# A graph network's gathered tiles: who begins them, who squares the mean, who adds the update products

## The reference

```python
msg = jnp.concatenate([h[src], h[dst]], axis=-1) @ Mw.T + Mb
s1 = jax.ops.segment_sum(msg, dst, num_segments=N)
s2 = jax.ops.segment_sum(msg * msg, dst, num_segments=N)
mx = jax.ops.segment_max(msg, dst, num_segments=N)
mn = jax.ops.segment_min(msg, dst, num_segments=N)
mean = s1 / degc
var = jax.nn.relu(s2 / degc - mean * mean)
std = jnp.sqrt(var + STD_EPS)
agg = jnp.concatenate([mx, mn, std, var], axis=-1)
h_neigh = jnp.concatenate([agg, agg * (logd / DELTA), agg * (DELTA / logd)], axis=-1)
u = jnp.concatenate([h, h_neigh], axis=-1) @ Uw.T + Ub
```

## Time and profile before

| | us |
|---|---|
| median of 3 runs | 1750.26 |
| lowest, highest | 1748.87, 1753.49 |
| span of the profiled execution | 2141.7 |

### The profile page before, as it was taken

How to read it: one execution, slowest core, us unless ns; L and a number is a source line. 1 busy time by engine, 2 the same in 40 slices (tenths; PEclk the granted TensorE clock), 3 DMA queues, 4 the chain that set the end, 5 groups by cost and what they waited for, 6 DMA issues and landing times. The chain is left out here.

```text
span 2141.7 us, 10446 instructions
## 1 busy us (share of the span) xinstructions
PE 682.6 (32%) x2156; PEld 402.8 (19%) x2156; DVE 1096.6 (51%) x2178; ACT 455.6 (21%) x1024; POOL 1235.7 (58%) x1358
## 2 busy tenths in 40 slices
PE   5611233132322470323132232362113322233265
PEld 5311121011111230112111111131101211112122
DVE  8600755464644843445464463572525664466464
ACT  0103321122111154111111111136101221112125
POOL 7673666676666127745675675406756666576504
PEclk9975666565655685566565666686556666656677
DMA  4363333333333033323332232204323333333200
GB/s 59 105 167 113 93 103 103 91 99 92 92 91 91 18 112 113 111 66 99 96 101 76 88 103 75 65 27 145 106 84 101 93 88 93 88 103 96 76 0 30
DMA packets 97107, 190.18 MB, mean 89 GB/s; under 512 B 30792, under 2 KB 56984, under 8 KB 97040
## 3 DMA queue, kind: packets, MB, share of 16 engines
q0 software_dynamic: 59968, 160.78, 26.6%
q1 hardware_dynamic: 37077, 28.77, 4.9%
HBM read 168.75 MB, written 17.75 MB: 87 GB/s over the span
## 5 line engine op out<-in xcount | busy, mean ns | idle before, releaser
L742 POOL DMA_INDIRECT G<-p_by_rank,index x774 | 734.8, 949 | 560.2 <-issue 227.8
L742 POOL DMA_INDIRECT G<-p_by_node,index x387 | 367.4, 949 | 225.0 <-issue 120.3
L921 PE MATMUL ps<-wide_ident,agg 128*128 128x128 f32 x288 | 80.3, 434 | 1209.3 <-issue 701.2
L1470 DVE TENSOR_TENSOR ps<-ps,G 128x1024 f32<-128x1024 f32 (+3 forms) x222 | 250.3, 1127 | 191.2 <-issue 78.4
L921 PEld LDWEIGHTS ps<-wide_ident,agg 128*128 128x128 f32 x288 | 51.5, 217 | 1239.5 <-issue 721.9
L936 PE MATMUL ps<-w_u_sb,aggT 128*128 128x384 f32 x576 | 284.3, 654 | 0.0
L1714 DVE SCALAR_TENSOR_TENSOR var<-tot,rdeg,msq 128x128 f32<-128x128 f32 x75 | 26.1, 348 | 426.4 <-ACT msq L1109 407.8
L936 PEld LDWEIGHTS ps<-w_u_sb,aggT 128*128 128x128 f32 x576 | 162.6, 282 | 144.7 <-issue 119.1
L1135 ACT ACTIVATE u_sb<-ps 128x128 f32<-128x128 f32 x75 | 20.7, 277 | 721.1 <-remote 509.0
L1472 DVE TENSOR_TENSOR ps<-ps,G 128x512 f32<-128x512 f32 (+3 forms) x222 | 141.6, 638 | 0.0
L1471 DVE TENSOR_TENSOR ps<-ps,G 128x512 f32<-128x512 f32 (+3 forms) x222 | 141.5, 637 | 0.0
(11 more groups left out here) (280 smaller groups left out, 1328.3 us busy)
## 6 DMA issues: line engine op xcount, KB each, us to landing
G<-p_by_rank,index POOLq DMA_INDIRECT x774
p_by_rank<-base SPq DMA_DIRECT2D x18, 512.0 KB
G<-p_by_node,index POOLq DMA_INDIRECT x387
p_by_node<-G SPq DMA_DIRECT2D x6, 514.0 KB
w_u_sb<-in_w_u SPq DMA_DIRECT2D x3, 768.0 KB
x_r<-rows_by_rank SPq DMA_DIRECT2D x1, 1600.0 KB
G<-shared_rows SPq DMA_DIRECT2D x12, 53.0 KB
windows<-src_pad SPq DMA_DIRECT2D x1, 624.8 KB, 14.1
```

Source lines behind the costliest of these rows:

```text
L742: g.indirect_dma_start(G[:, n % R, j, 0:w], None, table, bass.IndirectOffsetOnAxis(ap=named, axis=0))\
L921: ins = nc.tensor.transpose(ps[:, 2, i * D:(i + 1) * D], agg[:, t % 2, i * D:(i + 1) * D], ident[:, :])
L1470: TT(run[:, 0:nk, :], run[:, 0:nk, :], G[:, n % R, 0:nk, 0:2 * D], ALU.add)
```

## The change

The first two groups of each tile are now full, and no shared rows lie in them. DVE begins a tile when both have landed: one triple reads both groups from G and writes `run`, `top` and `low`. ACT's `begin` and `square_mean` are gone; DVE squares the mean in `variance`. ACT copies all three products, two of them with the degree's factor as scale (`scale_products`), and PE adds them as it turns them, in three accumulating products. `combine` is gone. The ring has 13 places, `agg` three buffers, the turned aggregates two banks of PSUM in turn, and the batch statistics of a tile come four tiles later, with the last ones after the last row. The single rows of the last tile gather in `base`, not in PSUM.

```diff
-        sizes = [GW] + [rest] * (rest > 0) + [GW] * (full - 1)
+        sizes = [GW] * 2 + [rest] * (rest > 0) + [GW] * (full - 2)
...
-            sh = 0 if t < T - 1 and j == 0 else min(left, nk)
+            sh = 0 if t < T - 1 and j <= 1 else min(left, nk)
...
-    R = 14
+    R = 13
+    NB = 3
...
+        def turned(t):
+
+            return ps[:, 5 if t % 2 and t > 4 else 2, :]
...
             def turn_update(l, t):
-                pe.wait_ge(u_ready.sem, u_ready.at(l, t + 1))
+                pe.wait_ge(z_copied.sem, z_copied.at(l, t + 1))
                 if t >= 1:
                     pe.wait_ge(u_copied.sem, u_copied.at(l, t))
-                nc.tensor.transpose(ps[:, 7, 0:D], u_sb[:, t % 2, :], ident[:, :]).then_inc(u_turned.sem, 1)
+                for i in range(3):
+                    ins = mm(u_ps, u_sb[:, t % 2, i * D:(i + 1) * D], ident[:, :], start=i == 0, stop=i == 2)
+                ins.then_inc(u_turned.sem, 1)
...
-            def begin(l, t):
-
-                n = tile_groups[t][0]
-                act.wait_ge(gathered[n % R].sem, gathered[n % R].at(l, slot_before[n]))
-                if n in brought:
-                    act.wait_ge(brought[n].sem, brought[n].at(l, transfers(n)))
-                if t:
-                    act.wait_ge(low_ready.sem, low_ready.at(l, t))
-                f(run, G[:, n % R, :, 0:2 * D], ACT.Copy)
-                f(top, G[:, n % R, :, 0:D], ACT.Copy)
-                f(low, G[:, n % R, :, 0:D], ACT.Copy).then_inc(begun.sem, 1)
...
-            def square_mean(l, t):
-                act.wait_ge(summed.sem, summed.at(l, t + 1))
-                if t >= 2:
-                    act.wait_ge(var_ready.sem, var_ready.at(l, t - 1))
-                f(msq[:, t % 2, :], tot[:, t % 2, 0:D], ACT.Square, scale=rdeg[:, t:t + 1]).then_inc(mean_sq.sem, 1)
...
-            def copy_product(l, t):
+                f(aggT[:, t % 2, :], turned(t), ACT.Copy).then_inc(agg_copied.sem, 1)
+
+            def scale_products(l, t):
                 act.wait_ge(z_done.sem, z_done.at(l, t + 1))
                 if t >= 2:
                     act.wait_ge(u_turned.sem, u_turned.at(l, t - 1))
-                f(u_sb[:, t % 2, :], ps[:, 4, 0:D], ACT.Copy).then_inc(z_copied.sem, 1)
+                f(u_sb[:, t % 2, 0:D], ps[:, 4, 0:D], ACT.Copy)
+                f(u_sb[:, t % 2, D:2 * D], ps[:, 4, D:2 * D], ACT.Copy, scale=amp[:, t:t + 1])
+                f(u_sb[:, t % 2, 2 * D:3 * D], ps[:, 4, 2 * D:3 * D], ACT.Copy, scale=att[:, t:t + 1])\
+                    .then_inc(z_copied.sem, 1)
...
                 if j == 1:
-                    dve.wait_ge(begun.sem, begun.at(l, t + 1))
-                else:
-                    dve.wait_ge(dve_used.sem, dve_used.at(l, n))
-                here = G[:, n % R, 0:nk, 0:D]
-                TT(run[:, 0:nk, :], run[:, 0:nk, :], G[:, n % R, 0:nk, 0:2 * D], ALU.add)
-                TT(top[:, 0:nk, :], top[:, 0:nk, :], here, ALU.max)
-                TT(low[:, 0:nk, :], low[:, 0:nk, :], here, ALU.min).then_inc(dve_used.sem, 2 if j == 1 else 1)
-                if j == 1:
-                    own_rows(l, n)
+                    begin(l, n)
+                    return
+                rows, here = G[:, n % R, 0:nk, 0:2 * D], G[:, n % R, 0:nk, 0:D]
+                before = 2 if j == 2 and t else 0 if j == 2 else 1
+                dve.wait_ge(ch.sem, ch.n - before)
+                ch.step(TT(run[:, 0:nk, :], run[:, 0:nk, :], rows, ALU.add))
+                dve.wait_ge(ch.sem, ch.n - before)
+                ch.step(TT(top[:, 0:nk, :], top[:, 0:nk, :], here, ALU.max))
+                if j == 2:
+                    dve.wait_ge(ch.sem, ch.n - before)
+                dve.wait_ge(dve_used.sem, dve_used.at(l, n))
+                TT(low[:, 0:nk, :], low[:, 0:nk, :], here, ALU.min).then_inc(dve_used.sem, 1)
+
+            def begin(l, n):
+                t = GROUPS[n][0]
+                a, b = n - 1, n
+                dve.wait_ge(gathered[a % R].sem, gathered[a % R].at(l, slot_before[a]))
+                if t:
+                    dve.wait_ge(summed.sem, summed.at(l, t))
+                    dve.wait_ge(low_ready.sem, low_ready.at(l, t))
+                ch.step(TT(run, G[:, a % R, :, 0:2 * D], G[:, b % R, :, 0:2 * D], ALU.add))
+                ch.step(TT(top, G[:, a % R, :, 0:D], G[:, b % R, :, 0:D], ALU.max))
+                TT(low, G[:, a % R, :, 0:D], G[:, b % R, :, 0:D], ALU.min).then_inc(dve_used.sem, 2)
+                if t == 0 or chunk_of[t] < chunk_of[t - 1]:
+                    dve.wait_ge(base_ready.sem, base_ready.at(l, NC - chunk_of[t]))
+                dve.wait_ge(ch.sem, ch.n - 1)
+                ch.step(TT(run[:, 0, :], run[:, 0, :], base[:, t, S1:S2 + 1, :].rearrange("p a d -> p (a d)"), ALU.add))
+                if t:
+                    dve.wait_ge(ch.sem, ch.n - 1)
+                    ch.step(TT(top[:, 0, :], top[:, 0, :], base[:, t, TOP, :], ALU.max))
+                    dve.wait_ge(dve_used.sem, dve_used.at(l, n + 1))
+                    ch.step(TT(low[:, 0, :], low[:, 0, :], base[:, t, LOW, :], ALU.min))
...
-                sums, most, least = ps[:, 5, 0:2 * D], ps[:, 5, 2 * D:3 * D], ps[:, 5, 3 * D:4 * D]
-                into = sums, most, least
-                if n == early_groups[0]:
-                    sums, most, least = (base[:, t, S1:S2 + 1, :].rearrange("p a d -> p (a d)"),
-                                         base[:, t, TOP, :], base[:, t, LOW, :])
+                sums, most, least = into = (base[:, t, S1:S2 + 1, :].rearrange("p a d -> p (a d)"),
+                                            base[:, t, TOP, :], base[:, t, LOW, :])
                 if n in END:
-                    dve.wait_ge(agg_turned.sem, agg_turned.at(l, t - 1))
+                    dve.wait_ge(agg_turned.sem, agg_turned.at(l, t - NB + 1))
                     dve.wait_ge(var_ready.sem, var_ready.at(l, t - 1))
-                    into = tot[:, t % 2, :], agg[:, t % 2, 0:D], agg[:, t % 2, D:2 * D]
+                    into = tot[:, t % 2, :], agg[:, t % NB, 0:D], agg[:, t % NB, D:2 * D]
...
             def variance(l, t):
-                dve.wait_ge(mean_sq.sem, mean_sq.at(l, t + 1))
-                ch.step(STT(var[:, t % 2, :], tot[:, t % 2, D:2 * D], rdeg[:, t:t + 1], msq[:, t % 2, :],
-                            ALU.mult, ALU.subtract))
-                ch.wait()
-                TS(agg[:, t % 2, 3 * D:4 * D], var[:, t % 2, :], 0.0, None, ALU.max).then_inc(var_ready.sem, 1)
-
-            def combine(l, t):
-                U, z = u_sb[:, t % 2, :], ps[:, 4, :]
-                dve.wait_ge(z_copied.sem, z_copied.at(l, t + 1))
-                ch.step(STT(U, z[:, D:2 * D], amp[:, t:t + 1], U, ALU.mult, ALU.add))
-                ch.wait()
-                STT(U, z[:, 2 * D:3 * D], att[:, t:t + 1], U, ALU.mult, ALU.add).then_inc(u_ready.sem, 1)
+                s1, s2 = tot[:, t % 2, 0:D], tot[:, t % 2, D:2 * D]
+                dve.wait_ge(summed.sem, summed.at(l, t + 1))
+                ch.step(STT(msq[:, t % 2, :], s1, rdeg[:, t:t + 1], s1, ALU.mult, ALU.mult))
+                ch.wait()
+                ch.step(TT(var[:, t % 2, :], s2, msq[:, t % 2, :], ALU.subtract))
+                ch.wait()
+                TS(agg[:, t % NB, 3 * D:4 * D], var[:, t % 2, :], rdeg[:, t:t + 1], 0.0, ALU.mult, ALU.max)\
+                    .then_inc(var_ready.sem, 1)
...
+                    if n in END and END[n] >= 4:
+                        statistics(l, END[n] - 4)
+                    if n == NG - 1:
+                        for t in range(T - 4, T):
+                            statistics(l, t)
```

More of the change, by code:

```diff
@@ L341, in build @@
         var = sb("var", [P, 2, D])
-        agg = sb("agg", [P, 2, 4 * D])
+        agg = sb("agg", [P, NB, 4 * D])
         aggT = sb("aggT", [P, 2, 4 * D])
-        u_sb = sb("u_sb", [P, 2, D])
+        u_sb = sb("u_sb", [P, 2, 3 * D])
         bstats = sb("bstats", [P, T, 6])
@@ L1140, in copy_update @@
                 act.wait_ge(u_turned.sem, u_turned.at(l, t + 1))
-                f(uT[:, hot(t)], ps[:, 7, 0:D], ACT.Identity, bias=v_sb[:, 5:6]).then_inc(u_copied.sem, 1)
+                f(uT[:, hot(t)], u_ps, ACT.Identity, bias=v_sb[:, 5:6]).then_inc(u_copied.sem, 1)
             def stage_a(l):
                 bases(l)
-                for n in range(NG + 3):
+                for n in range(NG + 1):
                     if l == 0 and n < NG:
                         keep_ranks(l, n)
-                    if n < NG and GROUPS[n][1] == 0 and GROUPS[n][0] < T - 1:
-                        begin(l, GROUPS[n][0])
-                    if n - 1 in END and END[n - 1] <= FAR:
[L1151 to L1175, removed]
@@ new lines, in stage_a @@
+                    if n in END:
+                        t = END[n]
+                        deviation(l, t)
+                        if t > FAR:
+                            copy_turned(l, t)
+                            scale_products(l, t)
```

(52 more changed lines are left out.)

46 lines of the change are left out of this document (11 added, 35 removed).

## The result

The changed kernel takes 1771.19 us (median of 4 runs, 1770.25 to 1775.34) against 1749.95 of the kernel before: ratio 1.0117, interval [1.0103, 1.013], 21 us slower. The forecast was 1785 in a range of 1752 to 1812: the direction and the mechanism came, the size of one term was too large.

The account below looks back on a forecast made before the run. The prediction took POOL's gather spacing, one per 1.25 us, as the bound. It added 29 + 4 + 1 + 1 = 35 us to the timed median of 1750.26, forecasting 1785 us, range 1752 to 1812 (own range 1771 to 1802).

Parts of the forecast that it names:

- POOL's spacing is the bound, and the profiled waits are not in the timed runs: Whole kernel: POOL issues one gather per 1.25 us almost without pause; the extra 391 us belong to the profiled execution alone.
- rival in which the waits were real: POOL's waits for DVE partly exist in timed runs, so the change frees the ring: 1737 to 1745 us; chance 0.09.
- Begin on DVE, 72 x 0.40 = 29: Start of 72 tiles: DVE triples with both inputs in SBUF lengthen gathers by 0.40 us each, 29 us.
- the sign that went by it: Changed timeline: 70 to 150 gathers starting inside L1464 to L1466 should take 1.2 to 1.9 us, excess about 29.
- The rival of the gathers that miss: At DVE's begin, landing puts triples between gather starts; 0.1 us or less each, total under 5, time 1753; chance 0.18.
- The even fall's 0.72 a triple: Begin triples: if gather starts fell evenly over 1.25 us, the three instructions would cost 0.48 + 0.12 + 0.12 us.
- The bounds of 0 and 78: Begin triples: 0 us if gathers always start outside, 78 if one starts with each triple's first instruction.
- Single rows, 4: Last tile's 78 single rows, accumulated in base with both inputs in SBUF: 0.05 us a row, 4 us.
- Variance, 1: Squaring the mean on DVE: an extra instruction with two SBUF inputs in 75 places costs 1 us.
- Products, +1 with the variance's exchange: Chain after each layer's last row, more ACT and PE instructions: +0.3 us a layer, +1 in all; bounds -1 and +3.
- Ring, 0: Ring of 13 instead of 14, at the start of a layer: taken as 0 us, bounds 0 and 11.
- What goes, nothing: Removed ACT begin and waits around ACT and DVE: gain only if timed runs wait there, at most 13 us.

Follow-up runs that it names:

- repeated profile: The kernel before, unchanged, profiled a second time: span 1753.9 us, measured 1755.61 us in that run.
- the begin alone: Kernel before with the first two groups full, DVE beginning from both and ACT's begin gone, all else kept: 1772.45 us, ratio 1.0117.
- short shift: Changed kernel plus an unread DVE reduction of 256 elements before each begin except a layer's first tile: 1797.32 us, ratio 1.0261 to the kernel before.
- long shift: Changed kernel plus an unread DVE reduction of 864 elements before each begin except a layer's first tile: 1769.4 us, ratio 1.0101.

## Why the prediction was right, and what was mis-sized

*POOL's spacing is the bound, and the profiled waits are not in the timed runs*: right. The repeated profile and the changed kernel's have no such waits, and the table's last column leaves them no room. The rival in which the waits were real would have needed the begin alone to be faster; it was slower by 18 to 23.

*Begin on DVE, 72 x 0.40 = 29*: the mechanism right, the size off. Measured are 72 x 0.25 = 17.9. This term was mis-sized, and with it the sign that went by it: 20 gathers of 1.2 us or more, where 70 to 150 were expected. The measured time stands at the low end of the forecast's own range, 1771, which was worked out with 0.2 a triple. 0.40 came from L1488 to L1490, triples whose first instruction has its gather anywhere from its start to its end; the begin waits for a landing, and the landing puts POOL's next gather mostly 0.98 into an instruction of 1.23.

That place can be worked out, as an estimate: in the changed kernel's trace a gather lands 2.8 us after its start (median), which is two spacings of 1.25 and 0.3, so the begin starts 0.3 after a gather has started, and the next gather 0.95 into the begin. The trace of before told no landing times. That the term was not further off is luck: it was read from the one odd execution, and in the repeated profile the same 12 triples carry 6.1 us, 0.51 each, which would have made 37.

The rival of the gathers that miss had the cause of this right, that the landing fixes the place, but the place is a hit, a short one. The short shift, with half of its gathers 0.48 to 0.55 into it, shows what a worse place would have cost: 41.4 us. The even fall's 0.72 a triple counted three instructions that catch gathers independently of each other; a begin catches one, since the gather that was held fixes the place of the next. The bounds of 0 and 78 held.

The Trainium skill's two sentences in "SBUF — State Buffer", section "Who interferes with whom", go apart here too: that a DVE instruction with two SBUF inputs contends with a GpSimd instruction reading SBUF agrees with every run (0.95 beside one input, 1.94 at 164.01 beside two); that tensor_tensor leaves transfers issued by GpSimd alone does not hold for these indirect gathers. The hold is what remains of VectorE's instruction when the gather starts, less 0.13 to 0.14 us.

*Single rows, 4*: 1.5 us, counted over the 20 gathers of the changed kernel that start inside L1577; its companions add 0.2. *Variance, 1*: 1.4 beside L1706, about what was said. Both are too small to be timed by themselves. *Products, +1 with the variance's exchange*: 0.35 in the chain on ACT and PE, in each of the three layers; the span less the gathers, with its spread of 3.5, cannot show it (617.6 against 617.7). *Ring, 0*: at most 3 us. *What goes, nothing*: right; ACT's busy time fell from 456.5 in the repeated profile to 326.5 without effect on the span.

Together: 29 + 4 + 1 + 1 was forecast, and 17.9 + 1.5 + 1.4 was found, with 1.3 more than in the repeated profile beside the triples at the layers' heads: some 22, against 21 in the timed runs.

## What to carry to other kernels

Where GpSimd issues gathers without a pause, look on VectorE for instructions with both inputs in SBUF: a gather that starts inside one is held for all but the last 0.13 us of it, whatever VectorE's own load, and what that costs depends on where in the instruction it starts. Put an accumulator or a copied operand into PSUM, even if VectorE then does more, as long as VectorE is not the bound; here 166 us more on VectorE gave back 18. And when a profile's span is far above the timed runs, take a tally of the timed runs from the spacing of the bounding engine before any wait of that profile is believed, or profile again.

## What the runs showed that was not expected

In the long shift a gather that starts in the very first hundredths of L1468, an instruction on two inputs, passes, and the instruction is a little longer. At 442.75 the gather starts 0.01 into L1468 and is not held; DVE's instruction takes 0.74 instead of 0.69. At 222.54, 0.07 into it, the gather is held for 0.48, and L1468 takes its 0.69. Of the 21 gathers of that trace that start inside L1468, the 12 up to 0.031 in take 0.94 to 0.95, beside 0.74 to 0.76 on DVE; the 9 from 0.034 on are all held, by 0.48 to 0.52.

A gather that already runs does not hold VectorE in the same way: 66 of the 72 begins of the changed kernel start while a gather runs, 0.18 us or more after its start, and take 1.22 to 1.23 like the others.

One execution of the kernel before spanned 2141.7 us under the profiler, another 1753.9, with the same program; what held the first up was not found.
